# A two-layer graph network on one core: diagonal-left blocks by seven products of quarters in place of eight

## The reference

```python
h = jnp.maximum(_layernorm(x, axis=-1), 0.0)
x = x + adj @ (h * (u >= 0.1) / 0.9)          # layer 1
h = jnp.maximum(_layernorm(x, axis=-1), 0.0)
x = x + adj @ (h @ W) + b                     # layer 2
```

## Time and profile before

| | |
|---|---|
| median of 3 runs | 921.59 us (921.55 to 923.07) |
| the profiled execution | 920.12 us; its span, first to last instruction, 918.3 us |
| granted TensorE clock | 1.000 |
| TensorE / VectorE / ScalarE / GpSimd busy | 98% / 26% / 5% / 0% of the span |
| read from HBM | 360.74 MB, 395 GB/s over the span |
| block loads | 339 of 1 MiB, 2 of half that |

### The profile page before, as it was taken

How to read it: one execution, slowest core, us unless ns; L and a number is a source line. 1 busy time by engine, 2 the same in 40 slices (tenths; PEclk the granted TensorE clock), 3 DMA queues, 4 the chain that set the end, 5 groups by cost and what they waited for, 6 DMA issues and landing times.

```text
span 918.3 us, 10443 instructions
## 1 busy us (share of the span) xinstructions
PE 900.0 (98%) x4488; PEld 415.4 (45%) x4488; DVE 234.5 (26%) x449; ACT 42.8 (5%) x120; POOL 2.6 (0%) x13
## 2 busy tenths in 40 slices
PE   6799999999999999999999999999999999999998
PEld 5445444444444444444444444444444444444443
DVE  5364732323203202030303021030220300300334
ACT  3100000000000000000000000000000000000000
POOL 1000000000000000000000000000000000000000
PEclk9999999999999999999999999999999999999999
DMA  8999999999999999999999999989999999999993
GB/s 348 421 420 420 422 420 422 420 421 421 421 420 421 420 421 420 421 419 421 403 419 379 410 367 380 399 339 369 385 353 382 371 386 419 390 390 389 412 422 149
DMA packets 52909, 363.53 MB, mean 396 GB/s; under 512 B 5728, under 2 KB 6016, under 8 KB 10752
## 3 DMA queue, kind: packets, MB, share of 16 engines
q1 hardware_dynamic: 52800, 362.83, 97.5%
q0 software_dynamic: 64, 0.03, 0.0%
HBM read 360.74 MB, written 2.10 MB: 395 GB/s over the span
## 4 chain that ended last, share of the span: by engine, by line
PE 92%; DMA 5%; SPq 2%; issue 0%; DVE 0%
PE banks L720 45%; PE row_sums L695 37%; PE banks L714 6%; DMA blocks<-in_adj 5%; PE banks L730 3%; SPq L464 1%; PE row_sums L704 1%; PE banks L807 0%; PE finished L772 0%; PE row_sums L772 0%; SPq L447 0%; SPq L446 0%; DVE x L654 0%
## 5 line engine op out<-in xcount | busy, mean ns | idle before, releaser
L720 PE MATMUL banks<-blocks,features 128*64 128x512 f32 x1912 | 665.2, 593 | 0.0
L695 PE MATMUL row_sums<-blocks,features 128*64 128x512 f32 x1696 | 547.1, 592 | 1.5 <-DMA blocks<-in_adj 1.5
L720 PEld LDWEIGHTS banks<-blocks,features 128*64 128x64 f32 x1912 | 221.3, 137 | 215.6 <-issue 215.1
L695 PEld LDWEIGHTS row_sums<-blocks,features 128*64 128x64 f32 x1696 | 192.7, 137 | 201.6 <-issue 196.4
L617 DVE TENSOR_TENSOR acc<-acc,banks 64x512 f32<-64x512 f32 (+1 forms) x112 | 76.8, 686 | 597.9 <-PE banks L720 540.7
L714 PE MATMUL banks<-blocks,features 128*64 128x512 f32 x224 | 98.1, 592 | 0.1
L524 ACT ACTIVATE turned<-finished 32x128 f32<-32x128 f32 (+1 forms) x68 | 17.8, 262 | 790.3 <-DVE finished L584 789.1
L730 PE MATMUL banks<-blocks,features 128*64 128x256 f32 x240 | 54.3, 379 | 0.1
L714 PEld LDWEIGHTS banks<-blocks,features 128*64 128x64 f32 x224 | 30.6, 137 | 29.0 <-issue 28.8
L730 PEld LDWEIGHTS banks<-blocks,features 128*64 128x64 f32 x240 | 32.8, 137 | 21.7 <-issue 8.5
L704 PE MATMUL row_sums<-blocks,features 128*64 128x256 f32 x256 | 30.5, 382 | 7.1 <-DMA blocks<-in_adj 7.1
(11 more groups left out here) (48 smaller groups left out, 97.0 us busy)
## 6 DMA issues: line engine op xcount, KB each, us to landing
blocks<-in_adj SPq DMA_DIRECT2D x339, 1024.0 KB, 13.0
out<-x SPq DMA_DIRECT2D x7, 256.0 KB, 3.6
x<-in_x SPq DMA_DIRECT2D x1, 1024.0 KB, 10.9
acc<-in_u SPq DMA_DIRECT2D x1, 1024.0 KB, 12.9
blocks<-in_adj SPq DMA_DIRECT2D x2, 512.0 KB, 25.1
x<-in_x SPq DMA_DIRECT2D x1, 768.0 KB, 7.2
acc<-in_u SPq DMA_DIRECT2D x1, 768.0 KB, 8.8
x<-in_x SPq DMA_DIRECT2D x1, 256.0 KB, 3.1
```

Source lines behind the costliest of these rows:

```text
L695: return nc.tensor.matmul(row_sums[at, t.unit % 2, nodes], features[:, tile_of(k, j), 0:D], tile, start=first and t.n == unit_first[t.unit ...
L720: return nc.tensor.matmul(banks[at, t.sum.bank, nodes], features[:, tile_of(t.k, j), D:2 * D], tile, start=t.n == t.sum.first and j == t.t ...
```

## The change

Blocks left of the diagonal from row 4 on, both layers at once, are done by a form of Strassen's method. A block is cut into quarters: two halves of its four source tiles times two halves of its 512 target nodes. The features of a half of the source tiles are a second matrix of two columns, layer 1 and layer 2. The 2 x 2 by 2 x 2 product of quarters, eight products, is made with seven. Each product is two matmuls of 256 columns, so an item has 14 matmuls of 256 columns in place of 8 of 512. For it, VectorE makes sums and differences of the block's quarters (three into `quarters`, one in place of A21), GpSimd makes four differences of feature tiles (`mixed`), two sets of each. The products of a whole row are summed in four banks (`SEVEN_BANKS`), and at the row's last seven VectorE adds them with sixteen additions of 64 x 256 (`TERMS`) to `x1` and `acc`. The banks for other sums become 2, the slots 15. The item (k+1, k) moves ahead of the pairs in the late queue, and the "seven" queue has a window of its own (3 us after the row's start to 6 before its end). Loads of sevens are issued two items earlier. A row's transpose goes into its own bank of `row_sums`.

```diff
-SLOTS = 16
+SLOTS = 15
-SUM_BANKS = 4
+SEVEN_FROM = 4
+SEVEN_LOAD, SEVEN_MADE, SEVEN_SETS = 2, 3, 2
+SUM_BANKS, SEVEN_BANKS = 2, 4
+TERMS = [(1, 0, 0, 0, 1), (1, 1, 0, 0, 1), (2, 0, 0, 0, 1), (2, 1, 0, 0, 1),
+         (1, 0, 1, 0, 1), (1, 1, 2, 1, 1), (2, 0, 2, 1, 1), (2, 1, 2, 1, 1),
+         (1, 1, 3, 0, 1), (2, 0, 1, 1, 1), (2, 1, 3, 0, 1),
+         (1, 1, 3, 1, 1), (2, 0, 2, 0, 1), (2, 1, 3, 1, 1),
+         (1, 1, 0, 1, -1), (2, 1, 1, 1, 1)]
...
-        self.steps = 2 if kind == "one" else len(tiles)
+        self.steps = 2 if kind == "one" else 3.5 if kind == "seven" else len(tiles)
...
+            begin, end = windows[n][0], max(total - windows[n][1], windows[n][0] + 1.0)
+            at = begin + (end - begin) * (done[n] + 0.5) / len(q)
...
-        return Item("both", [self.operand(s, k)], k, s, s + 1)
+        return Item("seven" if s >= SEVEN_FROM else "both", [self.operand(s, k)], k, s, s + 1)
...
-                items += merged([both, ones, again, late], ROW_LEAD)
+                items += merged([both, ones, again, late], [SEVEN_OFF, (0, 0), (0, 0), (ROW_LEAD, 0)])
...
+    loads.sort(key=lambda load: load.first - (SEVEN_LOAD if items[load.first].kind == "seven" else 0))
...
+    for n, t in enumerate(sevens):
+        t.nth, t.set = n, n % SEVEN_SETS
+        t.at = max(t.n - SEVEN_MADE, t.loads()[0].released, sevens[n - SEVEN_SETS].n if n >= SEVEN_SETS else 0)
...
+            for t in sevens:                                            # GpSimd
+                b11, b12, b21, b22 = (features_of(t, tiles, layer) for tiles in range(2) for layer in (1, 2))
+                pool.wait_ge(h2_ready, t.needs)
+                if t.nth >= SEVEN_SETS:
+                    pool.wait_ge(used, sevens[t.nth - SEVEN_SETS].n + 1)
+                nc.gpsimd.tensor_tensor(t1, b12, b11, ALU.subtract).then_inc(seven_mixed, 1)
+                nc.gpsimd.tensor_tensor(t3, b22, b12, ALU.subtract).then_inc(seven_mixed, 1)
+                pool.wait_ge(seven_mixed, 4 * t.nth + 1)
+                nc.gpsimd.tensor_tensor(t2, b22, t1, ALU.subtract).then_inc(seven_mixed, 1)
+                pool.wait_ge(seven_mixed, 4 * t.nth + 3)
+                nc.gpsimd.tensor_tensor(t4, t2, b21, ALU.subtract).then_inc(seven_mixed, 1)
...
+            def make_quarters(t):                                       # VectorE
+                a11, a12, a21, a22 = (quarter(t, nodes, tiles) for nodes in range(2) for tiles in range(2))
+                dve.wait_ge(block_arrived[t.loads()[0].slot], t.loads()[0].arrived)
+                if t.nth >= SEVEN_SETS:
+                    dve.wait_ge(used, sevens[t.nth - SEVEN_SETS].n + 1)
+                nc.vector.tensor_tensor(s1, a21, a22, ALU.add).then_inc(seven_made, 1)
+                dve.wait_ge(seven_made, 4 * t.nth + 1)
+                nc.vector.tensor_tensor(s2, s1, a11, ALU.subtract).then_inc(seven_made, 1)
+                dve.wait_ge(seven_made, 4 * t.nth + 2)
+                nc.vector.tensor_tensor(s4, a12, s2, ALU.subtract).then_inc(seven_made, 1)
+                nc.vector.tensor_tensor(a21, a11, a21, ALU.subtract).then_inc(seven_made, 1)
+
+            def add_seven(q):
+                dve.wait_ge(used, q.last + 1)
+                for n, (layer, nodes, bank, half, sign) in enumerate(TERMS):
+                    dve.wait_ge(sum_added, q.earlier + done.get((layer, nodes), 0))
+                    nc.vector.tensor_tensor(to, to, banks[half * D:(half + 1) * D, SUM_BANKS + bank, 0:HALF_BLK],
+                                            ALU.add if sign > 0 else ALU.subtract).then_inc(sum_added, 1)
...
                 if n in closing:
-                    add_sum(closing[n])
+                    (add_sum if closing[n].seven is None else add_seven)(closing[n])
+                for t in sevens:
+                    if t.at == n:
+                        make_quarters(t)
                 if n - 1 in unit_end:
                     unit_of_layer_1(unit_end[n - 1])
...
+            def seven(t):                                               # TensorE
+                pe.wait_ge(seven_mixed, 4 * t.nth + 4)
+                products(0, (a11, b11), (a22, t4))
+                pe.wait_ge(seven_made, 4 * t.nth + 1)
+                products(1, (a12, b21), (s1, t1))
+                pe.wait_ge(seven_made, 4 * t.nth + 3)
+                products(2, (s4, b22), (s2, t2))
+                pe.wait_ge(seven_made, 4 * t.nth + 4)
+                product(3, 0, s3, t3, 0, only=True)
+                return product(3, 1, s3, t3, 1, only=True)
```

More of the change, by code:

```diff
@@ L245, in plan @@
             load.until = n
+    sevens = [t for t in items if t.kind == "seven"]
+    loads.sort(key=lambda load: load.first - (SEVEN_LOAD if items[load.first].kind == "seven" else 0))
     free, holder, count = [-1] * SLOTS, [None] * SLOTS, [0] * SLOTS
-    for load in loads:
+    for n, load in enumerate(loads):
         load.slot = min(range(SLOTS), key=lambda q: free[q])
-        assert free[load.slot] < load.first, "a block needs a slot that is still held"
+        assert free[load.slot] < min(later.first for later in loads[n:]), "a block needs a slot that is still held"
         count[load.slot] += 1
@@ L292, in plan @@
         opened |= halves
-        done += 1 if q.ahead is None else 2
+        done += len(TERMS) if q.seven is not None else 1 if q.ahead is None else 2
         q.done = done
+        if q.seven is not None:
+            assert not q.opens
+            seven_done[q.seven] = done
         if q.ahead is not None:
             ahead_done[q.ahead] = done
-    bank_free, bank_of = [-1] * SUM_BANKS, [None] * SUM_BANKS
+    bank_free, bank_of = [-1] * (SUM_BANKS + SEVEN_BANKS), [None] * (SUM_BANKS + SEVEN_BANKS)
+    q_before = None
     for q in sums:
-        q.bank = min(range(SUM_BANKS), key=lambda b: bank_free[b])
+        if q.seven is not None:
+            q.before = q_before or max((r for r in bank_of[SUM_BANKS:] if r), key=lambda r: r.done)
+            q_before = q
+            continue
+        q.bank = min(range(SUM_BANKS if q.last >= sevens[0].n else len(bank_free)), key=lambda b: bank_free[b])
         assert bank_free[q.bank] < q.first, "more open sums than banks"
@@ L424, in final_banks, with quarter, features_of @@
         def final_banks(n):
-            return finished if n % 2 == 0 else row_sums
+            at = SUM_BANKS + n % 2 * 2
+            return banks[:, at:at + 2, :]
+        def quarter(t, nodes, tiles):
+            tile_rows = blocks[:, t.loads()[0].slot, :].rearrange("p (t n) -> p t n", n=BLK)
+            return tile_rows[:, tiles * 2:tiles * 2 + 2, nodes * HALF_BLK:(nodes + 1) * HALF_BLK]
+        def features_of(t, tiles, layer):
+            at = tile_of(t.k, 2 * tiles)
+            return features[:, at:at + 3:2, (layer - 1) * D:layer * D]
         def x1_half(s):
@@ L731, in layer_2_of_row_0, with product, products @@
                                      start=j == 0, stop=j == TILES - 1)
+            def seven(t):
+                a11, a12, s3, a22 = (quarter(t, nodes, tiles) for nodes in range(2) for tiles in range(2))
+                s1, s2, s4 = (quarters[:, t.set, n, :, :] for n in range(3))
+                b11, b12, b21, b22 = (features_of(t, tiles, layer) for tiles in range(2) for layer in (1, 2))
+                t1, t2, t3, t4 = (mixed[:, t.set, n, :, :] for n in range(4))
+                opens, closes = t.n == t.sum.first, t.n == t.sum.last
+                def product(bank, half, of, by, j, only=False):
+                    return nc.tensor.matmul(banks[half * D:(half + 1) * D, SUM_BANKS + bank, 0:HALF_BLK], by[:, j, :],
+                                            of[:, j, :], start=opens and (only or j == 0),
+                                            stop=closes and (only or j == 1))
+                def products(bank, left, right):
+                    for j in range(2):
+                        product(bank, 0, *left, j)
+                        product(bank, 1, *right, j)
+                pe.wait_ge(seven_mixed, 4 * t.nth + 4)
[7 more added lines that the diff above has]
+                return product(3, 1, s3, t3, 1, only=True)
             def lower(t, j):
```

88 lines of the change are left out of this document (51 added, 37 removed).

## The result

The changed kernel takes 936.43 us in the median (935.8 to 937.86), the kernel before 921.57 beside it: 1.0164 of it, 95% interval 1.0142 to 1.0186. It is slower, as forecast, but by 14.9 us where 6.1 were forecast (927.7 less 921.6).

What follows compares the result with a forecast made beforehand. TensorE was taken to bound the kernel, DMA close behind. Span 918.3 less 36.9 is 881.4; plus DMA 2, VectorE 31, GpSimd 10 gives 924.4, plus 3.3 to the median: 927.7 us, range 902 to 944.

Steps and rivals of the forecast that it cites:

- TensorE's part: In rows 4 to 15, 90 items of 14 narrower matmuls take 3.02 us for 3.43, saving 36.9 us.
- The floor: Span with TensorE's saving 881.4, plus 3.3 from span to median and 3.9 of waits after row 15: 888.6 us.
- DMA, +2: Block loads nearly bind, worst from row 2's end to mid row 6; slack elsewhere: 2 us lost, bounds 0 and 8.
- VectorE, +27: At row ends the third seven's set queues behind additions and chain: 31 us, of which 3.9 after row 15.
- GpSimd, +10: Four differences per seven, nearest row 0.287 us each, some colliding with VectorE: 10 us lost, between 0 and 21.
- The signs: Wrong if TensorE's idle time is ended by DMA, gaps come mid-row, or no gaps and a time near 887.
- Products no cheaper: TensorE's 256-column pairs run at 0.49 us instead of 0.432, so the 36.9 vanish: 951; chance 0.03.
- Full exclusion: VectorE and GpSimd take turns throughout, GpSimd's loss 21 us: time 939; chance 0.18 for this or more.
- VectorE hides: Third sevens' sets get through early or adds are shorter, TensorE or DMA stays the bound: 887 to 902; chance 0.17.

Runs made afterwards that it cites:

- e6: The changed kernel without GpSimd's differences and VectorE's sums of quarters, 15 slots, loads of sevens no longer issued two items early: 890.62 us.
- e3: The changed kernel without GpSimd's differences and without VectorE's sums of quarters, 15 slots: 898.55 us.
- e1: The changed kernel without GpSimd's four differences, the products taking plain features: 918.32 us.
- e2: The changed kernel without VectorE's sums of quarters, GpSimd's differences still made: 897.91 us.
- d0: The changed kernel, whole computation, with loads in the order of first use: 935.42 us.
- d3: The changed kernel with loads in order of first use, a new order of products, sevens 8 us after row start to 12 before end, from row 6: 905.21 us.
- c2: The changed kernel with sevens only in rows 8, 10, 11, 12, 15, late items by eight products, more sum banks, a narrower window: 922.35 us.
- c3: As c2, with sevens in row 9 too: 921.84 us.
- d4: As d3, but with the loads of sevens issued two items early again: 923.10 us.
- d2: The changed kernel with loads in order of first use, a new order of products, sevens 8 us after row start to 12 before end: 907.70 us.

## Why the prediction was wrong

The direction was right, and so were the places of the long waits at the row ends. In the sum two terms were too small (DMA and GpSimd), one was too large (VectorE), and the loss by the clock had no term at all. With `e6`, `e3` and `e1` between the forecast's floor and the changed kernel, the steps are 890.6 (e6, the floor), 7.9 (e3 less e6), 19.8 (e1 less e3) and 18.1 (changed less e1), together 936.4. The forecast had, on the same scale, 881.4 + 3.3 + 3.9 = 888.6, then 2, 27 and 10. So the miss of 8.7 us is +2.0, +5.9, -7.2 and +8.1, and the forecast would have been further off without the error that went the other way.

These steps add up by construction, and their sizes hang on the order in which things are taken away. Without VectorE's sums GpSimd's differences cost nothing (e2 is 0.6 under e3), so the 18.1 is a cost of the two together. In the changed kernel itself the order of loads is worth 1.0 us (`d0`) and not 7.9.

- *TensorE's part, 36.9.* Right. e6 ran at 1.000 clock with TensorE busy 865.0, 35.0 less than in the earlier trace rows.
- *The floor.* 890.6 for 888.6. The waits after row 15 were there: 0.86 and 2.50 for 3.9.
- *DMA, +2.* **The first step that failed**: 7.9 in the kernel without sums and differences. The worst stretch was found where it is (gaps of 2.17 at 250 us and 1.55 at 322 us in the changed kernel). What failed is the step that set the least work between a slot's release and its next use (6.9 us) against the shortest time from issue to landing (4.8, or 2.3 beyond the transfer), and so took the slack elsewhere, "0 to 3 us", as enough. In e3 the median time from 500 to 760 us was 8.6, and TensorE waited 0.4 to 1.1 us there in rows 11, 12 and 14. The upper bound of 8 was the value.
- *VectorE, +27.* 19.8 with GpSimd out of the way: the profiled executions of e1 and e3 differ by 11 us of idle time and 8 of busy time, and 5 to 7 of the latter are the clock. The places were right; the waits were shorter than forecast. Row by row, forecast and gap in the changed kernel, waits for a second result of the same set included: row 8, 3.4 and 4.70; row 10, 4.0 and 3.87; row 11, 1.7 and 2.25; row 12, 2.4 and 1.87; row 13, 1.8 and 0.88; row 14, 5.2 and 2.65; row 15, 7.8 and 6.11; after it 3.9 and 3.36. The sum is 30.2 for 25.7, and 6.3 of the 25.7 belong to GpSimd (next). In row 14 TensorE had already waited 0.99 for a block, at 727.8.
- *GpSimd, +10.* **The second step that failed**: 18.1. The nearest row (0.287 for a select of the same size) was too low a stand-in: alone a difference takes 0.45 to 0.46, four 1.8. Beside VectorE it takes up to 0.90, and the third seven of a run waited up to 0.84. Where the features come last, in rows 8 and 10, its four operations and the set start together: 4.70 and 3.87, which the forecast had put under VectorE, are 1.12 and 1.11 in e1 (waits for the features alone). So 6.3 of the 18.1 stand there, some 5 in the short waits, and 3.4 in the half rate behind the gaps of rows 8 and 10, which e1 does not have there. The rest, some 3, was not split; VectorE's sets, slowed from 0.69 to 0.75-0.80 an operation (28 us of its time), are the likely place.
- *The clock.* **A term that was missing**: 8.4 us in the profiled execution and 10.8 by the mean of the four (0.9885). That alone is about the miss of 8.7. The profile says the same in another way: TensorE's idle time grew by 38 us, where the forecast's terms of 2, 31 and 10 are 43, so the waits as a whole were not too small. Its busy time is 877.9 where the forecast has 900.0 - 36.9 = 863.1. Of these 14.8 us the clock is 8.4 and the smaller gain 1.9; 4.5 stay unexplained. In the steps above the clock's loss is contained. By the mean clocks of all executions (e6 0.9995, e3 0.997, e1 0.993, changed 0.9885) some 2, 4 and 4 us of it fall to the DMA, VectorE and GpSimd steps. A gap of one size doesn't always bring it: behind 2.44 us at 250 us the clock was at its lower level in e1 (0.57 from 251 to 255) and not in e3 (1.00), and behind the 2.50 after row 15 in e1 and e3 and not in the changed kernel (1.00). That may be one source of the spread between executions of a kernel; only one execution of each has a trace.
- *The signs.* Two of the signs that the prediction gave for being wrong came: gaps in the middle of rows (nine short waits for GpSimd, 5.2 us) and waits for blocks.
- *Rivals.* "Products no cheaper" is refuted by e3. "Full exclusion", 939 by its sum, came nearest to the time, and its 21 for GpSimd is nearer to 18.1 than the 10 that was taken; its 2 and 31 have the same errors as the forecast. The prediction says that it decides from about half of the collisions on. By its own numbers it is about a fifth: 37 less 33, of 21. "VectorE hides" needed other orders than the change has: `d3` is that case.

The Trainium skill (SBUF — State Buffer, "SBUF: two separate sides") says that a VectorE operation with two SBUF inputs and a GpSimd operation that reads SBUF exclude each other, the loser blocking fully. The trace bears it out in part. VectorE and GpSimd in the changed kernel, when a set and its differences start together:

```profile
401.49 0.82 DVE L677 TENSOR_TENSOR quarters<-quarters,blocks 128x512 f32<-128x512 f32 x1
401.73 0.90 POOL L551 TENSOR_TENSOR mixed<-features 128x128 f32<-128x128 f32 x1
402.35 0.83 DVE L679 TENSOR_TENSOR quarters<-blocks,quarters 128x512 f32<-128x512 f32 x1
402.59 0.90 POOL L553 TENSOR_TENSOR mixed<-features,mixed 128x128 f32<-128x128 f32 x1
...
409.98 0.46 POOL L551 TENSOR_TENSOR mixed<-features 128x128 f32<-128x128 f32 x1
```

GpSimd's operation takes 0.90 beside VectorE and 0.46 alone; VectorE's takes 0.82 to 0.94 for 0.69. Four and four took 3.6 us (400.77 to 404.34), where one after another they would need 2.7 + 1.8 = 4.5. One of each is started every 0.86 us, where alone VectorE's dependent operations follow at 0.72 and GpSimd's at 0.41, 1.13 together. They slow each other, mostly GpSimd, and by less than one whole operation each time.

What stays open: why a gap of one size is followed by the lower clock in one execution and not in another; why c2 (and by its time c3), with few row ends, kept 12 us of idle time (both ran with the early loads, which d4 shows to be dear there, and were not run without them); and how the gain of d2 splits between its three changes, as the window was not run with only one of the others. d3 still waits 7.2 us on L812: 2.5 after row 15 as in the changed kernel, the rest where two banks of pair sums stand behind a row's chain. More banks were not tried.

## What to carry to other kernels

When work is taken off the bounding engine and put on an idle one, its share of busy time says little: write out the helper's queue in order at the place where its longest jobs meet, and put what needs the last-finished helper result last in the consumer's item. Count the waits that stand behind each other together: here loads in order, a new order of products and a later window brought 1, 8 and -2 us alone (the window in a nearby form), and 31 in one version with sevens from row 6 on (0.984 of the kernel before). Loading some blocks early is paid by the others once slots are few: 8 and 18 us where little else held TensorE, 1 us where much did. The shortest time to landing is too kind a measure for the work that must lie between a slot's release and its next use. And a gap of the bounding engine can cost more than its length: behind the gaps of 3.9 to 6.1 us here, 1.7 to 3.4 us more went by the clock.

## What was not expected of the hardware

- Each of GpSimd's four subtractions of 128x128 float32 took 0.45 to 0.46 us alone, and 0.78 to 0.90 beside VectorE's operations on two SBUF inputs; VectorE's 0.69 became 0.82 to 0.94.
- Gaps of TensorE of 4.70, 3.87 and 6.11 us were followed by stretches at a granted clock of 0.55 to 0.56; a 256-column matmul record took 0.63 us there in place of 0.38. Around 2.5 us it went either way: 0.57 behind 2.44 in e1, 1.00 behind 2.44 in e3.
- Around the gap of 6.11 us DMA fell to 145 GB/s (815 to 822), as slots are released by TensorE's items. Behind the gap at 404.5 it was 335 GB/s, behind the one at 500.0 still 418.
